# One kernel, two layers of attention and feed-forward: the first two phases put in one block, and the expert's rows gathered instead of scattered

## The chip, the cores and the metric

The kernel runs on one core of a Trainium2 chip. The metric is the device time of one execution in microseconds (us). The kernel before takes 649.71 us, the median of three runs (648.31, 649.71 and 651.97).

## What is computed

The input is x of shape (16, 256, 128), 4096 tokens of 128 numbers, and four residual steps follow one another:

```python
x = x + _L0_attn_ref(_layernorm(x, axis=-1), ...)   # gated linear attention, 16 heads of 8
x = x + _L0_ffn_ref(_layernorm(x, axis=-1), ...)    # 8 experts, one per token, and a shared expert
x = x + _L1_attn_ref(_layernorm(x, axis=-1), ...)   # conv, silu, decaying state, gate
x = x + _L1_ffn_ref(_layernorm(x, axis=-1), ...)    # FP4-quantised gated feed-forward
```

The change is all in the second step. Its router picks one expert for each token, and the token enters that expert multiplied with the sigmoid of its score:

```python
scores_aE = x_aD @ router_DE
vals_aK, idx_aK = jax.lax.top_k(scores_aE, 1)
gates_Ea = jax.nn.sigmoid(masked_aE).T
routed_in_EaD = gates_Ea[:, :, None] * x_aD[None, :, :]
mid_EaF = silu(routed_in_EaD @ w1_eDF) * (routed_in_EaD @ w3_eDF)    # F = 352
routed_out_EaD = mid_EaF @ w2_eFD
shared_aD = silu(x_aD @ ws1_DF) * (x_aD @ ws3_DF) @ ws2_FD
out_aD = shared_aD + routed_out_EaD.sum(axis=0)
```

## The kernel before

Tokens lie in 32 tiles of 128 (one tile is 128 partitions by 128 numbers). The work is four functions, `phase_a` to `phase_d`, one after the other. Each opens an `nc.Block()`, in which every engine has its own list of instructions and semaphores order them; at the end of a block all engines and their DMAs have to be done before any engine goes on. There is no planner: the order on each engine is written out by hand. `run_skewed(engine, body, first, lo, hi, last)` issues `body(j)` for all j, the middle ones in a hardware loop. `done(engine, semaphore, j, n, per, ago)` waits until step j - ago has been counted.

`phase_a` (L193) does the attention and the second layer norm, one batch of 256 tokens (two tiles) per step of a software pipeline over 16 batches. In a step TensorE scores keys against queries (`products`, L821, into the four banks of `ps_a`), ScalarE, VectorE and GpSimd copy and mask them into `at` (`copied` L423, `masked` L540, `cut` L361), TensorE multiplies with the values (`values`, L745), and `finish` (L843 to L845) forms the output. Then the normed rows `xn2s` are made on ScalarE (`normed`, L432), copied to `xn2` by GpSimd (`copy_xn2`, L368), transposed to `xn2T`, and the router's scores of the batch are taken (`scores`, L727). At the end of its queue SyncE loads the weights of the next phases and stores zeros over the whole of `xg_dram`, 40 stores of 128 rows (L329).

`phase_b` (L924) does two things side by side. TensorE runs the shared expert over 8 groups of 512 tokens: three steps `f` of six matmuls of 512 columns (L188 to L190, into two buffers each of `ps_1` and `ps_3`), and `down`, 24 matmuls of 128 rows (L1147). ScalarE takes silu (L1032), VectorE the product (L1107). Meanwhile the tokens are sorted by expert. VectorE finds each token's expert as a one-hot row (L1067 to L1076), TensorE counts (`count_and_rank`, L1134 to L1137), VectorE turns counts into `pos`, the row at which each token lies when tokens are sorted by expert and each expert's part is padded to whole slots of 128 (L1083 to L1091; 40 slots). GpSimd multiplies each tile with its gate (`gated`, L994) and scatters its rows to `xg_dram` at `pos` with an indirect DMA (L1002), 32 tiles one after the other, and then waits for all of them (L1007). The expert weights `w13` are split into a high and a low part, `expert_high` on ScalarE (L1014) and `expert_low` on VectorE (L1061).

`phase_c` (L1173) runs the experts over 20 pairs of slots in 22 steps. SyncE loads the rows of a pair from `xg_dram` (L1221), two pairs ahead; TensorE transposes them (L1359), multiplies with w1 and w3 of the slot's expert (`up`, L188 to L190), transposes the product (L1389) and multiplies with w2 (L1367); VectorE copies out (L1311) and SyncE stores to `yg_dram` (L1225). GpSimd splits the weights of the next layer here (L1261 to L1267), and VectorE quantises weights in steps 1 to 3 (`prepare`). `phase_d` (L1397) gathers rows from `yg_dram` and adds them to x (L1493), and does the second layer.

Of the kernel before, what the change touches and what calls it, by code (L numbers as in the profile page):

```python
# [28 lines left out]
P = 128  # L29
# [49 lines left out]
def apart(eng):  # L79

    eng.nop(nofuse=True)
# [21 lines left out]
def constants():  # L103
# [13 lines left out]
            np.broadcast_to(EXPERTS - np.arange(EXPERTS, dtype=np.float32), (P, EXPERTS)),  # L117
        ],
# [10 lines left out]
def build(nc, io, out):  # L129
    ctx = ExitStack()  # L130
    with ctx:
# [3 lines left out]
        def sb(name, shape, dt=F32):  # L135
# [12 lines left out]
            "xg_dram": nc.dram_tensor("xg_dram", (SLOTS * P, D), F32, kind="Internal").ap(),  # L148
            "yg_dram": nc.dram_tensor("yg_dram", (SLOTS * P, D), F32, kind="Internal").ap(),
            "pos": sb("pos", [P, T], U32),  # L150
            "slot_expert": sb("slot_expert", [1, SLOTS], I32),
        }
        with ExitStack() as mid:
# [4 lines left out]
            g["small"] = sbm("small", [P, SLOTS + EXPERTS])  # L158
# [4 lines left out]
            with ExitStack() as early:  # L163
                def sbe(name, shape, dt=F32):
                    return early.enter_context(nc.sbuf_tensor(name, shape, dt))

                g["xn2"] = sbe("xn2", [P, T, D])
                g["xn2T"] = sbe("xn2T", [P, T * P])
                g["scores"] = sbe("scores", [P, EXPERTS, T])
                phase_a(nc, io, g)  # L170
                phase_b(nc, io, g)
# [13 lines left out]

def split_product(nc, to, left, right, start=True, stop=True):
# [6 lines left out]
def phase_a(nc, io, g):  # L193
    x, mask, ones, halves = g["x"], g["mask"], g["ones"], g["halves"]
    ident = mask[:, 2, :]
    with ExitStack() as ctx:
# [9 lines left out]
        ws = sb("ws", [P, 2, F])  # L206
        rope = sb("rope", [P, 2, N])
        block = sb("block", [P, P])
        wall = sb("wall", [P, 4 * P])
        wallp = sb("wallp", [P, 2, 4 * P], F32R)  # L210
        wload = sb("wload", [P, 2, P])
# [28 lines left out]
        zero = sb("zero", [P, D])  # L240
# [9 lines left out]
        xn2s = sb("xn2s", [P, 2, D])  # L250
        xn2t = sb("xn2t", [P, N])

# [4 lines left out]
        ps_m = bank("ps_m", [P, 512])  # L257

# [14 lines left out]
        s_xn2p, s_xn2t, s_xn2c, s_sc, s_scc = sem("s_xn2p"), sem("s_xn2t"), sem("s_xn2c"), sem("s_sc"), sem("s_scc")  # L273
# [16 lines left out]
        def _(sp):  # L290
# [17 lines left out]

            def body(j):
                done(sp, s_qs, j)  # L310
                apart(sp)
                done(sp, s_a, j, n=8, per=8, ago=2)
                if j.off == 0:
                    sp.wait_ge(s_zero, 2)
                for h in range(4):
                    sp.dma_start(qx[h::4, j.par, h, :, :].rearrange("p c n -> p (c n)"),
                                 qs[h::4, j.par, :, :].rearrange("p c n -> p (c n)")).then_inc(s_qx[j.par], 16)

            run_skewed(sp, body, 0, 2, 14, B - 1)

            sp.dma_start(g["small"][:, :], io["c_small"]).then_inc(g["s_w"], 16)
            for f, (f0, fn) in enumerate(FT):
                sp.dma_start(g["ws2"][0:fn, f, :], io["L0_ffn_ws2_FD"][f0:f0 + fn, :]).then_inc(g["s_w"], 16)
# [3 lines left out]
            sp.wait_ge(s_zero, 3)  # L327
            for s in range(SLOTS):
                sp.dma_start(g["xg_dram"][P * s:P * (s + 1), :], zero[:, :]).then_inc(g["s_w"], 16)  # L329
            sp.wait_ge(g["s_w"], 16 * (4 + 3 + SLOTS))  # L330

        @blk_.gpsimd
        def _(pool):
# [4 lines left out]
            nc.gpsimd.memset(zero[:, :], 0.0).then_inc(s_zero, 1)  # L338
# [24 lines left out]

            def copy_xn2(b):
                if not live(b):
                    return
                done(pool, s_xn2, b)
                nc.gpsimd.tensor_copy(g["xn2"][:, f_tiles(b), :], xn2s[:, :, :]).then_inc(s_xn2c, 1)  # L368
# [27 lines left out]
            def body(j):  # L396
                copy_xn2(j + -2)
# [11 lines left out]
            run_skewed(pool, body, -3, 3, 13, B + 1)  # L409

        @blk_.scalar
        def _(act):
# [5 lines left out]
            def copied(b, t, r):  # L418
# [4 lines left out]
                nc.scalar.activation(at[:, t, r, :, :], ps_a[:, r, :, :], ACT.Copy).then_inc(s_copied, 1)  # L423

# [83 lines left out]
            def body(j):  # L508
                copied(j, 1, 3)
                copied(j, 1, 1)  # L510
                normed(j + -1, xn2s, rstd2, shift2, s_nb2, (s_xn2p, s_xn2c), s_xn2)
# [7 lines left out]
                copied(j + 1, 0, 1)  # L519
                normed(j + 3, xn, rstd, shift, s_nb1, (s_xnTp,), s_xn)  # L520
# [4 lines left out]
            run_skewed(act, body, -3, 3, 13, B)  # L525

        @blk_.vector
        def _(dve):
# [128 lines left out]
            def body(j):  # L657
# [29 lines left out]
                lower(j + 1)  # L687

            run_skewed(dve, body, -2, 4, 14, B + 1)

            dve.wait_ge(s_ws, 32)
            nc.vector.tensor_copy(g["ws1"][:, 0, :, :], ws[:, :, :]).then_inc(s_prep_dve, 1)
            dve.wait_ge(s_prep_dve, 4)
            nc.vector.tensor_tensor(g["ws1"][:, 1, :, :], ws[:, :, :], g["ws1"][:, 0, :, :].bitcast(F32), ALU.subtract)

        @blk_.tensor
        def _(pe):
# [95 lines left out]
            def transposes2(b):  # L793
# [8 lines left out]
                for t in range(2):  # L802
                    last = nc.tensor.transpose(ps_t[:, tile(t)], xn2s[:, t, :], ident)
# [69 lines left out]
            run_skewed(pe, body, -2, 4, 14, B + 1)  # L873
# [50 lines left out]
def phase_b(nc, io, g):  # L924

    x, mask, ones = g["x"], g["mask"], g["ones"]
    scores, xn2, xn2T = g["scores"], g["xn2"], g["xn2T"]
    small, ws1, ws2 = g["small"], g["ws1"], g["ws2"]
    GROUPS, GT = T // 4, 4 * P
    with ExitStack() as ctx:  # L930
        def sb(name, shape, dt=F32):
            return ctx.enter_context(nc.sbuf_tensor("b_" + name, shape, dt))

        def sem(name):
            return ctx.enter_context(nc.semaphore("b_" + name))

        def bank(name, shape):
# [909 lines left out]
```

## Time and profile before

| | |
|---|---|
| median of three runs | 649.71 us |
| the profiled execution | 653.99 us, its span 652.3 us, mean granted clock of TensorE 0.936 |
| TensorE busy with matmuls | 551.6 us (85%) |
| TensorE busy with weight loads | 445.9 us (68%), beside matmuls |
| VectorE busy | 438.3 us (67%) |
| GpSimd busy | 355.2 us (54%) |
| ScalarE busy | 307.8 us (47%) |
| DMA | 28.12 MB, mean 43 GB/s |

The profile is one execution, taken by the hardware. Its times are counted from the start of the span. PE is TensorE (PEld its weight loads), DVE is VectorE, ACT is ScalarE, POOL is GpSimd, SP is SyncE; a q behind a name is the engine's sequencer or queue. A row of the timeline gives the start, the length, the engine, the line of the kernel, the operation, out<-in and how many were merged; a bracket at its end is how long the engine had been idle and who released it. Matmuls overlap one another, so that rates are read from starts, not from the length of one. The granted clock is a share of TensorE's full clock of 2.4 GHz; 0.50 is the level of 1.2 GHz.

### The profile page before, as it was taken

Reading aid. Unit: us, or ns where it says so; the run is one execution under the profiler, and the core shown is the slowest. Engines: PE = TensorE matmul, PEld = TensorE weight load, DVE = VectorE, ACT = ScalarE, POOL = GpSimd, SP = SyncE. Lnnn points to the kernel's source line nnn. Section 1 sums busy time; section 2 is a strip of 40 time slices with the busy share of each in tenths; the row PEclk is TensorE's granted clock in tenths of the full one; section 3 lists DMA queues with packets and bytes.
Section 4 is the critical chain, followed back from the end, with each engine's and each line's share of the span. In section 5 each row is a group of like instructions: output and inputs, shape, how many; then the busy total and the mean of one; then the engine's idle time right before and its main releaser. Section 6 shows DMA issues by size and latency. Waiting matters only on the chain. (4 is left out here: it accounts for less than half of the span.)

```text
span 652.3 us, 15280 instructions
## 1 busy us (share of the span) xinstructions
PE 551.6 (85%) x4468; PEld 445.9 (68%) x4469; DVE 438.3 (67%) x1172; ACT 307.8 (47%) x862; POOL 355.2 (54%) x550
## 2 busy tenths in 40 slices
PE   2799999999999379991799999278899999999965
PEld 1457676776776258871689999266778778778754
DVE  2678999999885155552284343126899899899883
ACT  1356666666574224430245444124545645655632
POOL 4468877878776248885400000445667767764221
PEclk9999999999999659996699999778899999999987
DMA  7000000000004551111422111110011011010000
GB/s 200 16 20 33 19 26 25 16 32 16 23 26 108 158 196 34 32 34 43 116 58 57 56 56 40 33 16 10 10 32 18 16 32 17 16 25 15 10 17 16
DMA packets 41686, 28.12 MB, mean 43 GB/s; under 512 B 5232, under 2 KB 38192, under 8 KB 41648
## 3 DMA queue, kind: packets, MB, share of 16 engines
q1 hardware_dynamic: 36016, 23.46, 12.2%
q0 software_dynamic: 5632, 4.20, 3.7%
q8 instruction: 19, 0.31, 0.2%
q14 instruction: 19, 0.16, 0.1%
HBM read 14.01 MB, written 9.44 MB: 36 GB/s over the span
## 5 line engine op out<-in xcount | busy, mean ns | idle before, releaser
L821 PE MATMUL a_ps_a<-a_qx,a_kt 32*128 32x512 f32 x512 | 70.8, 643 | 1.2 <-DMA a_qx<-a_qs 1.0
L1493 POOL DMA_INDIRECT x<-yg_dram,pos x32 | 58.1, 1815 | 11.9 <-issue 11.9
L895 POOL TENSOR_TENSOR d_hq<-d_fh_v,d_fh_scale 128x352 f32<-128x352 f32 x32 | 27.9, 889 | 57.6 <-DVE d_fh_v L921 57.6
L361 POOL TENSOR_SCALAR_AFFINE_SELECT a_at<-a_at 128x512 f32<-128x512 f32 x80 | 50.5, 650 | 11.8 <-ACT a_at L423 11.5
L1317 DVE TENSOR_TENSOR c_hid<-c_act,c_ps 128x352 f32<-128x352 f32 x40 | 20.7, 520 | 44.4 <-ACT c_act L1274 35.7
L423 ACT ACTIVATE a_at<-a_ps_a 128x512 f32<-128x512 f32 x80 | 44.5, 600 | 11.7 <-PE a_ps_a L821 10.1
L1498 POOL MEMSET d_hs<- 128x256 f32 x1 | 0.3, 311 | 88.3 <-POOLq L1177 88.3
L821 PEld LDWEIGHTS a_ps_a<-a_qx,a_kt 32*128 32x128 f32 x512 | 32.1, 192 | 17.9 <-issue 17.2
L1274 ACT ACTIVATE c_act<-c_ps 128x352 f32<-128x352 f32 x40 | 18.5, 463 | 49.6 <-PE c_ps L190 49.2
L1002 POOL DMA_INDIRECT xg_dram<-xn,pos x32 | 35.3, 1104 | 11.9 <-DVE pos L1091 6.2
L188 PE MATMUL d_ps_A<-d_xnT,wmix 128*128 128x256 f32 x128 | 38.4, 300 | 1.6 <-DVE d_xnT L1672 0.9
L540 DVE TENSOR_TENSOR a_at<-a_ps_a,mask 128x512 f32<-128x512 f32 x48 | 32.7, 684 | 8.6 <-PE a_ps_a L821 7.3
L190 PE MATMUL d_ps_A<-d_xnT,wmix 128*128 128x256 f32 x128 | 37.2, 290 | 0.0
L189 PE MATMUL d_ps_A<-d_xnT,wmix 128*128 128x256 f32 x128 | 37.2, 290 | 0.0
L745 PE MATMUL a_ps_o<-a_at,a_vpad 128*32 128x128 f32 x1024 | 34.6, 276 | 0.0
L1107 DVE TENSOR_TENSOR b_hid<-b_act,b_ps 128x512 f32<-128x512 f32 (+1 forms) x24 | 16.4, 683 | 25.8 <-ACT b_act L1032 25.8
L188 PE MATMUL c_ps<-w13p,c_xT 128*128 x80 | 30.8, 385 | 2.0 <-issue 1.0
L1032 ACT ACTIVATE b_act<-b_ps 128x512 f32<-128x512 f32 (+1 forms) x24 | 14.3, 596 | 38.4 <-PE b_ps L190 37.9
L1367 PE MATMUL c_ps_y<-w,c_hidT 128*128 (+1 forms) x240 | 31.6, 281 | 0.8 <-ACT c_hidT L1291 0.8
L393 POOL TENSOR_TENSOR a_kt<-a_e,a_rope 128x512 f32<-128x512 f32 x16 | 20.4, 1276 | 21.6 <-ACT a_e L447 21.6
L1367 PEld LDWEIGHTS c_ps_y<-w,c_hidT 128*128 128x128 f32 (+1 forms) x240 | 28.3, 191 | 3.0 <-issue 1.9
L1816 PEld LDWEIGHTS d_ps_G<-d_wd,d_hqT 128*128 128x128 f32 (+1 forms) x192 | 23.8, 199 | 8.6 <-issue 5.5
(274 smaller groups left out, 1807.3 us busy)
## 6 DMA issues: line engine op xcount, KB each, us to landing
a_qx<-a_qs SPq DMA_DIRECT2D x64, 64.0 KB, 1.9
b_w<-in_L_ffn_w_eDF_dram SPq DMA_DIRECT2D x2, 1408.0 KB, 8.1
xg_dram<-a_zero SPq DMA_DIRECT2D x40, 64.0 KB, 1.6
c_rows<-xg_dram SPq DMA_DIRECT2D x20, 128.0 KB, 2.1
yg_dram<-c_y SPq DMA_DIRECT2D x20, 128.0 KB, 1.8
out_dram<-x SPq DMA_DIRECT2D x16, 128.0 KB, 1.9
w<-in_L_ffn_w_eFD_dram SPq DMA_DIRECT2D x2, 512.0 KB, 5.1
x<-in_L_attn_x_dram SPq DMA_DIRECT2D x1, 768.0 KB, 5.7
```

The source lines that it names most:

```text
L188: nc.tensor.matmul(to, left(0), right(0), start=start, stop=False)
L189: nc.tensor.matmul(to, left(0), right(1), start=False, stop=False)
L190: return nc.tensor.matmul(to, left(1), right(0), start=False, stop=stop)
L361: nc.gpsimd.affine_select(at[:, t, r, :, :], at[:, t, r, :, :], pattern=[[0, 4], [1, P]], compare_op=ALU.is_ge, fill=0.0, base=0, channel_ ...
L423: nc.scalar.activation(at[:, t, r, :, :], ps_a[:, r, :, :], ACT.Copy).then_inc(s_copied, 1)
L540: nc.vector.tensor_tensor(at[:, t, r, :, :], ps_a[:, r, :, :], mask[:, 0:1, :].to_broadcast([P, 4, P]), ALU.mult).then_inc(s_masked, 1)
L745: last = nc.tensor.matmul(ps_o[32 * r:32 * r + 32, tile(t)], vpad[:, b.par, t, c0:c0 + 32], at[:, t, r, h, :], start=(t == 0 and h == 0), ...
L821: last = nc.tensor.matmul(ps_a[:, r, :, :], kt[rows, b.par, c_, tile(t)], qx[rows, b.par, :, c_, tile(t)], start=(c_ == 0), stop=(c_ == 1))
L895: return eng.tensor_tensor(self.by(to), self.by(self.v[:, :]), self.spread(self.scale), ALU.mult)
L1002: nc.gpsimd.indirect_dma_start(out=g["xg_dram"][:, :], out_offset=bass.IndirectOffsetOnAxis(ap=g["pos"][:, t:t + 1], axis=0), in_=xn2[:, t ...
L1367: last = nc.tensor.matmul(ps_y[:, t, :], hidT[0:fn, f.par, t, n, :], w2[0:fn, e_out[t], n, :], start=(n == 0), stop=(n == 2))
L1493: nc.gpsimd.indirect_dma_start(out=x[:, t, :], out_offset=None, in_=g["yg_dram"][:, :], in_offset=bass.IndirectOffsetOnAxis(ap=g["pos"][:, ...
```

## The change

- `phase_a` and `phase_b` become one function, `phase_ab`, in one block. The three last steps of the attention pipeline are written out by hand, with the first groups of the shared expert between them (`up(n, f)` is one step of the six matmuls, `down(n, half)` half of the 24). The shared expert uses PSUM banks and SBUF of the attention again: `ps_1` and `ps_3` are `ps_a`, the routing tables lie in `kt` and `qs`, the expert weights (a ring of five) in `at`.
- `xg_dram`, its 40 stores of zeros, the tiles' gating and the scatter are gone. In their place the normed rows are stored as they are, unsorted, to `xn2_dram` by SyncE, one store of 256 rows per batch from one of two buffers `xn2s`; GpSimd's copy to `xn2` goes.
- A table says which token lies in each place of each slot. VectorE splits `pos` into slot and place, and compares both against constants, which gives one-hot matrices `slot_high` (32 tiles by 40) and `slot_low` (32 tiles by 128, in four parts). GpSimd multiplies `slot_high` with the gate and with the token's number. 32 products on TensorE (`slots`) sum them to `slot_token` and `slot_gate` for the 40 slots.
- `gather` fetches the 256 rows of a pair with two indirect DMAs from GpSimd, into one of four buffers `rows`: pairs 0 to 3 in `phase_ab`, pairs 4 to 19 in `phase_c`. There VectorE multiplies them with `slot_gate` into the old two buffers before TensorE's transposes. VectorE's loop in `phase_c` is written out. SyncE loads no rows.
- `expert_low` goes from VectorE to GpSimd. The split of the shared expert's weights on VectorE goes from the end of `phase_a` to its step 3.

```diff
+def gather(nc, g, k):
+    for t in range(2):
+        nc.gpsimd.indirect_dma_start(
+            out=g["rows"][:, k % 4, t, :], out_offset=None, in_=g["xn2_dram"][:, :],
+            in_offset=bass.IndirectOffsetOnAxis(ap=g["slot_token"][:, 2 * k + t:2 * k + t + 1], axis=0),
+        ).then_inc(g["s_rows"][k % 4], 16)
...
     @blk_.sync
+            def store(b):
...
+                done(sp, s_xn2, b)
+                sp.dma_start(xn2_rows[:, f_tiles(b), :], xn2s[:, b.par, :, :]).then_inc(s_xn2s[b.par], 16)
...
             def body(j):
+                store(j + -4)
...
-            for s in range(SLOTS):
-                sp.dma_start(g["xg_dram"][P * s:P * (s + 1), :], zero[:, :]).then_inc(g["s_w"], 16)
...
     @blk_.gpsimd
-                copy_xn2(j + -2)
...
+            expert_low(0)
+            pool.wait_ge(s_pos, 1)
...
+            nc.gpsimd.tensor_tensor(slot_high[:, :, SLOTS:], slot_high[:, :, 0:SLOTS],
+                                    gate.unsqueeze(2).to_broadcast(by_slot), ALU.mult).then_inc(s_one, 1)
...
+            nc.gpsimd.tensor_tensor(slot_high[:, :, 0:SLOTS], slot_high[:, :, 0:SLOTS],
+                                    small[:, SLOTS + EXPERTS + P:].unsqueeze(2).to_broadcast(by_slot), ALU.mult).then_inc(s_part, 1)
+            for e_ in range(1, 4):
+                expert_low(e_)
+            pool.wait_ge(s_tab, 2)
...
+            for k in range(2):
+                gather(nc, g, k)
+            for e_ in range(4, EXPERTS):
+                expert_low(e_)
+            for k in range(2, 4):
+                gather(nc, g, k)
...
     @blk_.scalar
...
+            gated_up(0, 0)
+            squares(Seq(B - 1))
+            gated_up(0, 1)
+            gated_up(0, 2)
+            gated_up(1, 0)
+            scored(Seq(B - 2))
+            normed2(Seq(B - 1))
...
     @blk_.vector
...
+            for n in range(2, GROUPS):
+                for f in range(3):
+                    hidden(n, f)
+                    if f == 0 and n + 1 < GROUPS:
+                        token_low(n + 1)
+                    if (n, f) == (2, 2):
+                        positions()
+                    if (n, f) == (3, 0):
+                        slot_rows()
+                    if (3, 1) <= (n, f) <= (4, 1):
+                        slot_places(3 * n + f - 10)
+                    if (n, f) == (4, 2):
+                        slot_experts()
+                    if (n, f) == (5, 1):
+                        slot_table()
+                add(n - 1)
...
     @blk_.tensor
...
+            transposes2(Seq(B - 2))
+            up(0, 0)
+            values(Seq(B - 1), 1)
+            up(0, 1)
+            finish(Seq(B - 1))
+            up(0, 2)
+            up(1, 0)
+            scores(Seq(B - 2))
+            down(0, 0)
+            up(1, 1)
+            down(0, 1)
+            transposes2(Seq(B - 1))
+            up(1, 2)
+            scores(Seq(B - 1))
+            up(2, 0)
+            down(1, 0)
+            up(2, 1)
+            count_and_rank()
+            down(1, 1)
+            up(2, 2)
+            group(3)
+            group(4)
+            for part in range(4):
+                slots(part)
+            group(5)
...
 def phase_c(nc, io, g):
...
     @blk_.gpsimd
+            def rows_for(k):
+                done(pool, s_rg, Seq(k), ago=4)
+                gather(nc, g, k)
...
     @blk_.vector
+                if live(j + 2):
+                    k = j + 2
+                    dve.wait_ge(g["s_rows"][k.off % 4], 32 * (k.off // 4 + 1))
+                    done(dve, s_xp, k, ago=2)
+                    for t in range(2):
+                        c0 = 2 * k.off + t
+                        last = nc.vector.tensor_scalar(rows[:, k.par, t, :], g["rows"][:, k.off % 4, t, :],
+                                                       g["slot_gate"][:, c0:c0 + 1], None, ALU.mult)
+                    last.then_inc(s_rg, 1)
```

## Rows read from the trace of the kernel before

**Rows 1.** By stage: length, busy PE PEld DVE ACT POOL, clock, DMA share, GB/s.

```profile
27.00:197.00 170.00, 165.41 (x1929) 117.84 (x1929) 148.59 (x386) 109.06 (x320) 129.34 (x235) 1.00 0.06 23
209.90:232.20 22.30, 7.61 (x96) 6.01 (x93) 5.89 (x17) 6.38 (x17) 6.88 (x17) 0.67 0.58 153
232.20:242.60 10.40, 10.23 (x26) 7.24 (x26) 6.96 (x16) 2.61 (x5) 4.07 (x6) 0.55 0.78 273
242.60:297.10 54.50, 52.80 (x318) 43.70 (x318) 29.82 (x46) 21.53 (x36) 48.67 (x54) 1.00 0.11 33
297.10:309.80 12.70, 0.03 (x1) 0.03 (x1) 1.49 (x2) 0.00 (x0) 5.88 (x8) 0.59 0.15 46
309.80:323.00 13.20, 8.70 (x31) 7.16 (x31) 2.72 (x6) 2.80 (x7) 4.07 (x3) 0.63 0.53 144
323.00:413.00 90.00, 86.37 (x612) 79.88 (x610) 41.90 (x84) 40.86 (x134) 3.35 (x2) 1.00 0.18 50
```

**Rows 2.** Timeline where phase_a ends and phase_b begins.

```profile
208.25 20.87 SPq L329 DMA_DIRECT2D xg_dram<-a_zero  x40
209.91 0.61 PE L727 MATMUL a_ps_m<-a_router,a_xn2t 128*128 128x8 f32 x4
...
215.24 0.60 PE L843 MATMUL a_ps_m<-ones,a_sq 128*128 128x1 f32 x4 [0.99 <-ACT a_sq L478]
...
230.80 0.60 DVE L1067 TENSOR_REDUCE b_best<-scores 128x32 f32<-128x256 f32 x1 [10.46 <-PEq L196]
...
231.68 1.28 ACT L1032 ACT_TABLE_LOAD   x1
...
232.17 0.79 PE L188 MATMUL b_ps<-b_tokens,ws 128*128 128x512 f32 x1 [7.19 <-DVE b_tokens L1055]
```

**Rows 3.** Timeline where phase_b ends and phase_c begins, and its last product.

```profile
294.11 2.94 PE L1147 MATMUL b_ps_y<-ws,b_hid 128*128 128x128 f32 x24 [1.40 <-DVE b_hid L1107]
...
302.38 0.96 POOL L1002 DMA_INDIRECT xg_dram<-xn,pos  x1 [0.30 <-issue]
307.71 0.88 SPq L1221 DMA_DIRECT2D c_rows<-xg_dram  x2
...
309.77 0.69 PE L1359 MATMUL c_ps_t<-mask,c_rows 128*128 128x128 f32 x2 [12.72 <-DMA c_rows<-xg_dram]
...
324.44 1.50 PE L1367 MATMUL c_ps_y<-w,c_hidT 128*128 x12
...
410.38 1.60 PE L1367 MATMUL c_ps_y<-w,c_hidT 128*128 x12 [0.83 <-ACT c_hidT L1291]
...
414.73 0.31 POOL L1498 MEMSET d_hs<- 128x256 f32 x1 [88.30 <-POOLq L1177]
```

**Rows 4.** Costliest groups of the page: the indirect DMAs of GpSimd, scatter and gather.

```profile
L1493 POOL DMA_INDIRECT x<-yg_dram,pos x32 | 58.1, 1815 | 11.9 <-issue 11.9
...
L1002 POOL DMA_INDIRECT xg_dram<-xn,pos x32 | 35.3, 1104 | 11.9 <-DVE pos L1091 6.2
```

**Rows 5.** Timeline of the shared expert: the same half of down in two groups.

```profile
279.84 1.60 PE L1147 MATMUL b_ps_y<-ws,b_hid 128*128 128x128 f32 x12
...
286.98 1.60 PE L1147 MATMUL b_ps_y<-ws,b_hid 128*128 128x128 f32 x12
```

**Rows 6.** Instructions of single lines: ns min/median/max, first and last start, forms.

```profile
L895 POOL TENSOR_TENSOR d_hq<-d_fh_v,d_fh_scale x32: 777/889/1002, 463.7 to 644.3; 128x352 f32<-128x352 f32 x32
...
L895 DVE TENSOR_TENSOR wq<-c_w_v,c_w_scale x1: 1326/1326/1326, 336.6 to 336.6; 128x1120 f32<-128x1120 f32 x1
...
L1267 POOL TENSOR_TENSOR wmix<-c_wtap,wmix x1: 2927/2927/2927, 323.5 to 323.5; 128x1280 fp32r<-128x1280 f32 x1
```

**Rows 7.** Timeline: one scan on VectorE beside GpSimd's multiply, and one without.

```profile
192.29 1.29 POOL L393 TENSOR_TENSOR a_kt<-a_e,a_rope 128x512 f32<-128x512 f32 x1 [0.77 <-ACT a_e L447]
...
192.64 1.21 DVE L603 TENSOR_TENSOR_SCAN a_c<-ones,a_de,a_e 128x128 f32<-128x128 f32 x1
...
194.28 0.48 DVE L603 TENSOR_TENSOR_SCAN a_c<-ones,a_init,a_e 128x128 f32<-128x128 f32 x1
```

More of the change, by code:

```diff
@@ L151, in build @@
             "slot_expert": sb("slot_expert", [1, SLOTS], I32),
+            "slot_token": sb("slot_token", [P, SLOTS], U32),
+            "slot_gate": sb("slot_gate", [P, SLOTS]),
+            "rows": sb("rows", [P, 4, 2, D]),
+            "s_rows": [sem(f"s_rows{n}") for n in range(4)],
         }
@@ new lines, in _ @@
+            done(dve, s_x2, Seq(B - 1))
+            norm_stats(Seq(B - 1), stats2, s_st2)
+            norm_aggr(Seq(B - 1), stats2, mv2, s_st2, s_nb2, s_ln2)
+            hidden(0, 2)
+            hidden(1, 0)
+            hidden(1, 1)
+            add(0)
+            token_low(2)
+            hidden(1, 2)
+            one_hot()
+            for n in range(2, GROUPS):
+                for f in range(3):
+                    hidden(n, f)
+                    if f == 0 and n + 1 < GROUPS:
+                        token_low(n + 1)
[10 more added lines that the diff above has]
+                add(n - 1)
@@ L696, in _ @@
+            add(GROUPS - 1)
         @blk_.tensor
@@ new lines, in group, with count_and_rank @@
+            def group(n):
+                for f in range(3):
+                    up(n, f)
+                    if f < 2:
+                        down(n - 1, f)
+            def count_and_rank():
+                pe.wait_ge(s_hot, 2)
+                to = ps_r.rearrange("p e t -> p (e t)")
+                nc.tensor.matmul(ps_n, ones[:, :], hot[:, :, T - 1], start=True, stop=False)
+                nc.tensor.matmul(ps_n, ones[:, :], before[:, :, T - 1], start=False, stop=True)
+                nc.tensor.matmul(to, mask[:, 1, :], padded[:, 1:], start=True, stop=False)
+                nc.tensor.matmul(to, ones[:, :], before.rearrange("p e t -> p (e t)"),
+                                 start=False, stop=True).then_inc(s_r, 1)
@@ new lines, in slots @@
+            def slots(part):
+                if part == 0:
+                    pe.wait_ge(s_part, 1)
+                pe.wait_ge(s_pos, part + 2)
+                for t in range(8 * part, 8 * part + 8):
+                    last = nc.tensor.matmul(ps_s, slot_low[:, t, :], slot_high[:, t, :], start=(t == 0), stop=(t == T - 1))
+                if part == 3:
+                    last.then_inc(s_tab, 1)
+            run_skewed(pe, body, -2, 4, 14, B - 2)
+            scores(Seq(B - 3))
+            values(Seq(B - 1), 0)
```

530 lines of the change are left out of this document (269 added, 261 removed).

## Prediction

> **What bounds the kernel now.** I read the busy time by stage first. From 27 to 197 us and from 323 to 413 us TensorE is busy 97% and 96% of the time at full clock: the attention and the experts are bound by TensorE, and so is the shared expert between 242.6 and 297.1 (52.8 of 54.5) [rows 1]. Between these stand two seams where it hardly works. In the first, from 209.9 to 232.2, it is busy for 7.6 us of 22.3, and then runs at a clock of 0.55 until 242.6. In the second it does nothing for 12.7 us (297.1 to 309.8) and then has 8.7 us of work in 13.2, at 0.63 [rows 1].
>
> The timeline says who holds each seam. In the first, VectorE has long been idle when it starts phase_b at 230.80, 10.5 us after its last work: SyncE is storing zeros until 208.25 + 20.87 = 229.1, and the block can't end before they land. The first matmul of phase_b is at 232.17 [rows 2]. In the second, TensorE is done at 294.11 + 2.94 = 297.05, while GpSimd issues its last scatter at 302.38 and the next block starts at 307.71; the first transpose waits 12.7 us, and the first product with w2 (step 2 of phase_c) comes at 324.44 [rows 3]. GpSimd's 32 scatters take 1.10 us each with 0.37 us before them [rows 4], and the 32 multiplies by the gate lie between; that chain is longer than TensorE's part of phase_b.
>
> **First seam and shared expert.** Both kernels have the same work on TensorE up to the router product at 209.91 [rows 2]. I add what it has to do from there. What is left of the attention was 7.61 us of busy time at a mean clock of 0.67 [rows 1]; part ran at the lower level, and I take 6.5. A group of the shared expert takes 286.98 - 279.84 = 7.14 us [rows 5]; eight are 57.1, and the last half waits 1.4 for VectorE [rows 3]. Phase_b took 297.05 - 232.17 = 64.9 us, which is 6.4 more than 57.1 + 1.4; 10.4 us at 0.55 cost 4.7 of that [rows 1], and 1.7 are counting and waits, which stay. New are the 32 products of the slot table. A float32 product runs as two instructions here: 64 instructions, as 24 take 2.94 us [rows 3] 0.12 each, at most 7.8; they move 80 columns and not 128, so 7.5. Together 74.2 us.
>
> To this come stalls. The last batch is still a chain over four engines; now matmuls lie between its links, but `finish` stands in TensorE's queue ahead of `up(0, 2)` and waits for ScalarE's square, as it does before for 0.99 us [rows 2]; I count three such waits (the normed rows, the square, the one-hot rows) at 1.2 us, 3.6. `Square` and `Tanh` now stand between two `Silu`. Before, one table load of 1.28 us does for the change from one to the other [rows 2]. The reload for the gate's tanh (two loads, 2.6 us) falls beside VectorE's `positions`, which is longer: nothing. If the square needs one too, it costs up to 2.6 us.
>
> The second stall is VectorE in groups 3 and 4. Its usual work is 29.82 us in 54.5 [rows 1], 3.9 a group, 3.0 without `expert_low`. It gets `positions` (12 small operations, an estimate of 3.4), `slot_rows` with 1280 elements and four `slot_places` with 1024, which by the 1.33 us of a spread multiply of 1120 elements [rows 6] are 1.5 and 1.2 each. That is 2 x 3.0 + 3.4 + 1.5 + 4.9 = 15.8 us against TensorE's 14.3, which alone costs 1.5. Beside it GpSimd does two multiplies of 1280 elements, 2.9 us each [rows 6]. A scan on VectorE that meets GpSimd's multiply takes 1.21 us and 0.48 without it, ending with it (193.85 and 193.58) [rows 7], so VectorE can lose anything from 0 to 5.8. I take 3, and 4.5 for this stall. `slots` waits for the last part. The Trainium skill, page "SBUF — State Buffer", section "Who interferes with whom", says that a VectorE instruction with two inputs in SBUF and a GpSimd instruction that reads SBUF exclude each other for the whole instruction; the trace agrees for this scan. By that rule the whole 5.8 us would be lost, and the sum would be 2.8 us higher.
>
> TensorE so ends at 209.9 + 74.2 + 3.6 + 4.5 = 292.2, against 297.05.
>
> **Is GpSimd done by then?** After the table it issues four gathers, four `expert_low` and four more gathers. A gather without adding is not in the trace. The nearest rows are the scatter, 1.10 + 0.37 = 1.47, and the gather that adds, 1.82 + 0.37 = 2.19 [rows 4]; I take 1.6, nearer to the one that doesn't add. `expert_low` has 704 elements, between 0.89 us for 352 and 2.93 for 1280 [rows 6], 1.66. 12.8 + 6.6 = 19.4 us stand against TensorE's 14.3 + 2.9 + 1.4 and some 3 of group 5's start, 21.6: done 2 us before it, or at 2.19 each 2.5 us after it.
>
> **Second seam.** No scatter has to end, and the pairs' rows are there. After TensorE VectorE adds the last group, 0.7 us (1.49 us for two operations there [rows 1]), then the block ends. The end of a block with indirect DMAs cost 307.71 - 303.34 = 4.4 us [rows 3], part of it the wait for the last scatter; the one to phase_d comes 2.7 us after the last product, with a copy and a store in it [rows 3]. Bounds are 0 and 4.4; I take 2. Phase_c starts at 295.0 instead of 307.7.
>
> From there to the first product with w2 it was 16.7 us [rows 3]. TensorE's work in it is 8.70 us at 0.63, 5.5 at full clock [rows 1]; with the multiply by the gate, a transpose and two copies ahead of it 7.5 us at full clock, and 13 at 0.50. In the second seam before, a mean of 0.59 over 12.7 us [rows 1] means that the upper level held for 2.3 us after the last matmul; the new gap is about 4 us, so I expect a fall, and take 11.5. Step 2 then begins at 306.5 instead of 324.4: 17.9 us earlier.
>
> **Third phase.** A pair takes (410.38 - 324.44) / 19 = 4.52 us [rows 3]. GpSimd's two gathers are 3.2 us of it (4.4 at the dearest price), and it may run four pairs ahead; its 7.4 us of other work [rows 1] fits in that lead. VectorE is busy 41.9 of 90 us [rows 1], 2.1 a pair, and gets two multiplies, some 0.5. If a gather is late, VectorE waits for it, and behind it in its queue stand `prepare` and the next pair's copies, so TensorE two steps later. I take 0, up to 3 for a gather late at the start. SyncE's loads go at no gain: at pairs other than the first they were hidden. The last phases are as they were.
>
> **First phase.** Off go 16 copies on GpSimd (busy 129 of 170 us) and on come 16 stores in SyncE's queue ahead of the queries' DMAs, whose data are older by then; VectorE (149 of 170) gets the shared weights' split, 1.4 us, in step 3. TensorE is busy 165 of 170 [rows 1], so these can move it by some -2 to +2; I take 0.
>
> **Sum.** The profiled execution took 653.99 us with a span of 652.3, 4.3 above the median of 649.71. The saving is taken off both: span 634.4, execution 636.1, median 631.8.
>
> **The rivals.** *A clean seam:* VectorE keeps up (-4.5), the clock stays up at the start of phase_c (-4), the block's end costs 0.5 (-1.5): 27.9 saved, 621.8. For it speaks that VectorE and GpSimd have few common operations with two inputs; against it the 15.8 us against 14.3.
>
> *The seam is only moved:* the whole of GpSimd's multiplies is lost (+2.8), the square's table load (+2.6), gathers at 2.19 and 4.4 us for the block's end (2.5 + 4.4 behind TensorE's end instead of 2.8: +4.1), phase_c's start at the lower level (+1.5): 6.9 saved, 642.8. The scan's row speaks for the first of these, the 4.4 us for the third.
>
> *Slower:* phase_c becomes bound by GpSimd's 32 gathers. From 295 to the end of the last product at 412.0 are 117 us; less 7.4 of other work it breaks even at 3.4 us a gather (it begins to bind at 2.9). At 4.0 it would be 7.4 + 128 = 135.4 us, 18.4 more than before: 668. The trace's dearest is 2.19. The same page warns, in "SBUF: two separate sides", that GpSimd can't write descriptors while VectorE runs a copy-like operation in a two-port mode, and the new multiply by the gate is one. No row here shows it on an indirect DMA; by it a gather would wait for at most a 0.5 us multiply.
>
> **How the numbers follow.** My forecast has 0.53, the clean seam 0.18, the moved seam 0.20, the slower case 0.05; 0.04 are left for something not seen. The range goes from the clean seam to a little beyond the moved one: 621 to 645. A measurement of this kernel can tell 0.5% (3.3 us) from no change. Faster by more: 0.88, within: 0.05, slower: 0.07.
>
> **What would show it.** TensorE's last product with ws2 near 292 (284 if there were no stalls); the matmuls of `slots` close together for some 7.5 us; `slot_places` over 1.3 us where they meet GpSimd's multiplies; a gather of 1.1 to 1.8 us; phase_c's first transpose at about 296 and its first w2 product at 306; TensorE's clock near 1.00 from 210 to 290; pairs of 4.52 us. The prediction is wrong if a gather takes 3 us, or if TensorE in phase_c waits for `rows`.

## The result, and the profile after

The changed kernel takes 663.64 us (median of 4 runs, 662.30 to 664.89) against 650.84 for the kernel before (4 runs): a ratio of 1.021, 95% interval 1.018 to 1.023. It is slower by 13 us, where 18 us less were forecast. The profiled execution took 662.30 us with a span of 660.6, which is 8.3 us above the span of the kernel before; the other 4.5 of the 13 us are spread between executions (the profiled one is the shortest of its four, and that of the kernel before, at 653.99, is longer than all four runs beside it), and the account below is one of the two profiled spans.

The stage windows are read first, as in [rows 1]. Columns: stretch, its length, busy time of PE, PEld, DVE, ACT and POOL, granted clock, DMA share, GB/s.

```profile
27.00:197.00 170.00, 165.47 (x1928) 117.84 (x1929) 149.33 (x388) 108.89 (x320) 125.42 (x222) 1.00 0.09 32
209.90:232.20 22.30, 20.53 (x175) 16.81 (x173) 12.53 (x27) 11.72 (x25) 4.87 (x14) 1.00 0.58 159
232.20:290.00 57.80, 52.00 (x324) 44.18 (x323) 36.95 (x54) 17.53 (x30) 28.26 (x19) 0.97 0.10 29
290.00:305.80 15.80, 8.71 (x47) 7.06 (x46) 6.18 (x17) 3.88 (x11) 6.63 (x9) 0.89 0.46 119
305.80:420.30 114.50, 87.28 (x604) 77.73 (x602) 48.53 (x113) 40.32 (x129) 34.39 (x30) 1.00 0.16 37
```

The first phase is as it was. The first seam is gone: TensorE is busy 20.5 of its 22.3 us at full clock, where it had been busy 7.6. The loss is in the last line. The third phase has the same work for TensorE, 87.3 us against 86.4, but 114.5 us to do it in and not 90. The clock is 1.00 there, so it isn't the clock.

The timeline at the second seam answers to [rows 3]. Columns: start, length, engine, line, operation, and the idle time before it with what ended it.

```profile
287.96 2.94 PE L1176 MATMUL a_ps_o<-ws,a_hid 128*128 128x128 f32 x24 [1.40 <-DVE a_hid L876]
288.08 0.94 POOL L193 DMA_INDIRECT rows<-xn_dram,slot_token  x1 [0.30 <-issue]
290.94 0.69 DVE L880 TENSOR_TENSOR x<-x,a_ps_o 128x512 f32<-128x512 f32 x1 [2.44 <-PE a_ps_o L1176]
291.92 0.53 POOL L1367 MEMSET c_wraw<- 128x512 f32 x1 [2.90 <-POOLq L211]
...
292.64 0.44 PE L1484 MATMUL c_ps_t<-mask,c_rows 128*128 128x128 f32 x2 [1.74 <-DVE c_rows L1439]
...
305.81 1.50 PE L1492 MATMUL c_ps_y<-w,c_hidT 128*128 x12
```

The shared expert ends at 290.90, phase_c starts at 291.92 and the first product with w2 is at 305.81, 18.6 us earlier than the 324.44 of before. Up to here the change gave what was forecast.

From there the products with w2 show the loss. These are rows of one period of the third phase, from the transposes of one step to those of the next:

```profile
375.49 0.44 PE L1484 MATMUL c_ps_t<-mask,c_rows 128*128 128x128 f32 x2 [1.50 <-DVE c_rows L1439]
375.70 0.94 POOL L193 DMA_INDIRECT rows<-xn_dram,slot_token  x1 [4.23 <-DVE c_rows L1439]
375.77 1.51 PE L1492 MATMUL c_ps_y<-w,c_hidT 128*128 x12
...
379.89 0.32 PE L203 MATMUL c_ps<-w13p,c_xT 128*128 x1
380.25 0.46 ACT L1389 ACTIVATE c_act<-c_ps 128x352 f32<-128x352 f32 x1 [0.23 <-PE c_ps L203]
380.74 0.52 DVE L1432 TENSOR_TENSOR c_hid<-c_act,c_ps 128x352 f32<-128x352 f32 x1 [1.10 <-ACT c_act L1389]
381.18 0.48 DVE L1439 TENSOR_SCALAR c_rows<-rows,slot_gate 128x128 f32<-128x128 f32 x2
381.79 0.43 PE L1484 MATMUL c_ps_t<-mask,c_rows 128*128 128x128 f32 x2 [1.58 <-DVE c_rows L1439]
```

TensorE works from 375.49 to 380.21 and then stands for 1.58 us. What it stands for is a chain over three engines that starts with its own last matmul: ScalarE's silu, VectorE's product, VectorE's two multiplies by the gate, and only then the transposes of pair j+2. The waits of TensorE between 300 and 415 us (in total, times, longest) say how much that is:

```profile
PE c_ps_t L1484 <- DVE c_rows L1439: 28.2, 18, 2.1
```

The forecast's measure of a pair was (last product - first) / 19: it is (418.92 - 305.81) / 19 = 5.95 us now and was 4.52, so the 19 take 27.2 us more, and 16 of the 18 waits lie in them. The other two, 1.50 us each at 300.27 and 305.54, stand ahead of the first w2 product, so the waits account for 28.2 - 3.0 = 25.2 of the 27.2 us; where the other 2.0 lie is not settled. The first 16 periods take (407.25 - 305.81) / 16 = 6.34 us; in the kernel before, with the 17th product at 398.75, they took (398.75 - 324.44) / 16 = 4.64. The last three have no transposes ahead of them, and take 4.25, 4.33 and 3.09 us, as they did before:

```profile
394.73 1.60 PE L1492 MATMUL c_ps_y<-w,c_hidT 128*128 x12
401.02 1.51 PE L1492 MATMUL c_ps_y<-w,c_hidT 128*128 x12
407.25 1.53 PE L1492 MATMUL c_ps_y<-w,c_hidT 128*128 x12
411.50 1.60 PE L1492 MATMUL c_ps_y<-w,c_hidT 128*128 x12
415.83 1.60 PE L1492 MATMUL c_ps_y<-w,c_hidT 128*128 x12
418.92 1.60 PE L1492 MATMUL c_ps_y<-w,c_hidT 128*128 x12 [0.83 <-ACT c_hidT L1406]
...
423.28 0.31 POOL L1623 MEMSET d_hs<- 128x256 f32 x1 [39.16 <-POOLq L1293]
```

The account closes: 18.6 us won up to the first w2 product, 27.2 lost in the third phase, and from the start of phase_d 660.6 - 423.28 = 237.3 us against 237.6. That is a span of 652.3 - 18.6 + 27.2 - 0.3 = 660.6.

### The profile page after: what moved, and what is told of

It reads as the page before. It is cut to its first block and busy times, and to the rows that moved or that the text cites. A ratio compares the mean times of both kernels' runs of the same rounds, so it can differ in the third digit from the quotient of the medians.

```text
span 660.6 us, 15223 instructions
## 1 busy us (share of the span) xinstructions
PE 555.4 (84%) x4532; PEld 448.4 (68%) x4533; DVE 455.0 (69%) x1215; ACT 308.1 (47%) x862; POOL 351.6 (53%) x519
## 5 line engine op out<-in xcount | busy, mean ns | idle before, releaser
L193 POOL DMA_INDIRECT rows<-xn_dram,slot_token x40 | 40.2, 1004 | 61.2 <-DVE c_rows L1439 45.8
L1432 DVE TENSOR_TENSOR c_hid<-c_act,c_ps 128x352 f32<-128x352 f32 x40 | 20.8, 521 | 46.2 <-ACT c_act L1389 46.2
L525 ACT ACTIVATE a_at<-a_ps_a 128x512 f32<-128x512 f32 x80 | 44.5, 599 | 11.5 <-PE a_ps_a L1097 9.9
L1097 PEld LDWEIGHTS a_ps_a<-a_qx,a_kt 32*128 32x128 f32 x512 | 32.0, 192 | 17.7 <-issue 17.1
L1389 ACT ACTIVATE c_act<-c_ps 128x352 f32<-128x352 f32 x40 | 18.6, 464 | 49.7 <-PE c_ps L203 49.7
L1484 PE MATMUL c_ps_t<-mask,c_rows 128*128 128x128 f32 x40 | 8.7, 300 | 31.3 <-DVE c_rows L1439 31.3
L651 ACT ACTIVATE a_act<-a_ps_a 128x512 f32<-128x512 f32 (+1 forms) x24 | 14.3, 595 | 43.5 <-PE a_ps_a L203 43.5
L876 DVE TENSOR_TENSOR a_hid<-a_act,a_ps_a 128x512 f32<-128x512 f32 (+1 forms) x24 | 16.4, 682 | 25.8 <-ACT a_act L651 25.7
L462 POOL TENSOR_TENSOR a_kt<-a_e,a_rope 128x512 f32<-128x512 f32 x16 | 20.4, 1277 | 21.6 <-ACT a_e L561 21.6
```

What stands on the lines that cost most here:

```text
L193: nc.gpsimd.indirect_dma_start(out=g["rows"][:, k % 4, t, :], out_offset=None, in_=g["xn2_dram"][:, :], in_offset=bass.IndirectOffsetOnAxi ...
L1097: last = nc.tensor.matmul(ps_a[:, r, :, :], kt[rows, b.par, c_, tile(t)], qx[rows, b.par, :, c_, tile(t)], start=(c_ == 0), stop=(c_ == 1))
```

## The experiments

The theory, the ring: at the end of VectorE's step j, the multiply for pair j+2 stands behind the two products of pair j, and TensorE's step j+1 begins with the transposes of pair j+2. So the latency of silu, product and multiply is paid on TensorE once a pair. The rival, cost: the multiplies, or the gathers that they wait for, are simply more work than the third phase has room for. It was the forecast's own "slower" case, with gathers of over 2.9 us.

**The multiply ahead of the products.** The same instructions, in another order. Two further kernels, below, have each multiply twice (once into a buffer that nobody reads), in the late and in the early place.

```
-                if live(j):
-                    for t in range(2):
-                        done(dve, s_act, j, n=t + 1, per=2)
-                        ...
                 if live(j + 2):
                     ...
                     last.then_inc(s_rg, 1)
+                if live(j):
+                    for t in range(2):
+                        done(dve, s_act, j, n=t + 1, per=2)
+                        ...
```

> The changed kernel with one edit: in the third phase VectorE multiplies the rows of pair j+2 by the gate ahead of its two products of pair j instead of behind them. Theory (the wait): behind the products the multiply closes a ring from one step to the next, up(j,1) on TensorE, silu on ScalarE, product and multiply on VectorE, and then the transposes that stand first in TensorE's next step; in the trace of the changed kernel the transposes wait 31.3 us for the multiply, and a pair takes (418.92 - 305.81) / 19 = 5.95 us instead of 4.52. Moved ahead, a pair should be back at 4.5 to 4.6 us, the transposes should wait under 5 us in all, and the time should fall by some 27 us from 663.6, to 636. Rival (the gathers): GpSimd's indirect DMAs, their descriptors or their landing hold the pairs up, and the multiply only passes that on; then a pair stays near 5.9 us and the time within 3 us of 663.6.

Measured: 637.59 us (4 runs, 635.37 to 639.81) beside 651.42 for the kernel before, ratio 0.978 (0.973 to 0.983). In the trace the transposes' wait is nearly gone, and 11 pairs in a row (331.66 to 382.02) take 4.58 us each. Here are the same row of the waits and the dearest early step; columns of the second as in the timeline above:

```profile
PE c_ps_t L1484 <- DVE c_rows L1433: 4.9, 2, 3.5
```

```profile
320.01 3.29 POOL L1380 TENSOR_TENSOR wmix<-c_wtap,wmix 128x1280 fp32r<-128x1280 f32 x1
...
320.57 3.92 DVE L1260 TENSOR_TENSOR wq<-c_w_v,c_w_scale 128x1120 f32<-128x1120 f32 x1
...
325.60 0.44 PE L1484 MATMUL c_ps_t<-mask,c_rows 128*128 128x128 f32 x2 [3.55 <-DVE c_rows L1433]
```

The w2 products take 398.24 - 305.63 = 92.6 us against 113.1 in the changed kernel and 85.9 before: the order gave back 20.5 of the 27.2 us, where the theory had all of them. (The medians differ by 26, but the two spans by 660.6 - 638.0 = 22.6.) What is left is `prepare`: three of its operations stand in VectorE's queue in one step, and one of 1.33 us [rows 6] takes 3.92 beside GpSimd's multiply of 3.29. The first four pairs took 5.87, 6.03, 8.34 and 5.79 us.

**Each multiply twice, late.**

```
                     for t in range(2):
                         c0 = 2 * k.off + t
+                        nc.vector.tensor_scalar(spare[:, t, :], g["rows"][:, k.off % 4, t, :],
+                                                g["slot_gate"][:, c0:c0 + 1], None, ALU.mult)
                         last = nc.vector.tensor_scalar(rows[:, k.par, t, :], ...
```

> The changed kernel with the gate's multiply of each pair done twice in its late place (the first time into a spare buffer): 0.5 us more of VectorE's work a pair. Theory (the wait): it lies on the ring, so each pair takes 0.45 to 0.55 us more, 6.4 to 6.5, and the time is some 9 us above 663.6. Rival (the gathers): VectorE is busy 48.5 of 114.5 us in the third phase and has room; a pair stays at 5.95 and the time within 2 us.

Measured: 675.50 us (one run), 12 above the changed kernel. The first 16 periods of the w2 products (309.24 to 419.55) take 6.89 us each against 6.34 in the changed kernel (305.81 to 407.25): 0.55 us more, for two multiplies of some 0.24 us. Over 16 that is 8.8, the 9 that the theory had; another 3.4 us lie ahead of the first product, where the theory had none.

**Each multiply twice, early.** The same lines in the early place.

> The early multiply of e1_early, done twice. Theory (the wait): ahead of the products it lies beside TensorE's first half of the step and off the ring, so the second multiply costs nothing: a pair within 0.1 us of e1_early's and the time within 2 us of it. Rival (VectorE is simply too busy in the third phase, wherever the multiply stands): a pair takes 0.3 us or more longer than in e1_early and the time is 5 us or more above it.

Measured: 637.63 us (one run), the same as with single multiplies. Ten pairs (332.10 to 377.83) take 4.57 us. This one execution flatters it: its shared expert ended 4.8 us earlier than in the kernel with single multiplies (last product at 282.85 against 287.64), in code that is the same in both. Measured on the w2 products alone, the doubling costs 95.7 - 92.6 = 3.1 us, all of it in the early pairs, where VectorE is full. So the same extra half microsecond a pair costs 0.55 us of each period in one place and nothing in the other, once `prepare` is over. The cost theory falls. Each of these two kernels ran once, so this reading rests on the stretches inside their traces.

**The ring in the kernel before.** To see it without the gathers and without the joined block, the kernel before got it alone: SyncE loads a pair into an extra buffer, and VectorE copies it (a multiply by 1.0) into the buffer that TensorE transposes, at the end of its step or ahead of the products.

```
-                sp.dma_start(rows[:, j.par, :, :], ...
+                sp.dma_start(rows_in[:, j.par, :, :], ...
...
+                if live(j + 2):
+                    k = j + 2
+                    dve.wait_ge(s_rows[k.par], k.half(16, 16))
+                    done(dve, s_xp, k, ago=2)
+                    for t in range(2):
+                        last = nc.vector.tensor_scalar(rows[:, k.par, t, :], rows_in[:, k.par, t, :], 1.0, None, ALU.mult)
+                    last.then_inc(s_rg, 1)
```

> The kernel before, with SyncE's loads of rows as they are, but into a buffer of their own, from which VectorE copies each pair in two operations of 128x128 at the end of its step j (for pair j+2), the place that the gate's multiply has in the changed kernel. No gather, no merged block. Theory (the wait): the copy alone makes the ring; a pair takes 5.9 to 6.0 us and the time rises by some 27 us, from 650.8 to 678. Rival (the gathers, or anything else of the change in the third phase): the copy is 0.5 us of work on an engine busy 2.1 of 4.5 us a pair, so a pair stays at 4.5 to 4.6 and the time within 3 us of 650.8.

> The kernel before with VectorE's copy of the rows as in e4_before_copy_late, but ahead of the two products of the step. Theory (the ring is made by the place, not by the work): a pair in the steady part takes 4.5 to 4.6 us, as in the kernel before, and the time is within 3 us of 651.4. Rival (an operation more on VectorE and a buffer more between load and transposes cost wherever they stand): a pair takes over 5 us and the time is 10 us or more above it.

Measured: the late copy 681.11 us (4 runs), ratio 1.047 (1.043 to 1.052), the early one 655.13 (8 runs), ratio 1.006 (1.003 to 1.009). The w2 products take 110.5 us with the late copy (328.69 to 439.19) and 86.2 with the early one (323.74 to 409.98), 85.9 before. One wait of each period with the late copy, and TensorE's total (300 to 415 us, of which 13.1 are the seam):

```profile
378.15 1.60 PE L1376 MATMUL c_ps_y<-w,c_hidT 128*128 x12
...
384.04 0.44 PE L1368 MATMUL c_ps_t<-mask,c_rows 128*128 128x128 f32 x2 [1.38 <-DVE c_rows L1325]
384.32 1.52 PE L1376 MATMUL c_ps_y<-w,c_hidT 128*128 x12
```

```profile
PE c_ps_t L1368 <- DVE c_rows L1325: 40.6, 18, 13.1
```

A copy of 0.35 us for a pair, put in that place, makes a period of 4.64 us one of 6.18 (328.69 to 427.53, 16 of them) in a kernel that has nothing else of the change. Of the 29.7 us that the late copy costs, 24.6 lie in the w2 products and 4.3 ahead of the first (328.69 against 324.44). The early copy came out 4 us above the kernel before, a little more than the 3 expected; the third phase of its profiled execution has only 0.3 of that, and where the rest lies isn't settled.

**`prepare` spread out.** On top of the early multiply, one operation of `prepare` for each step and not three.

```
-                if 1 <= j.off < LO:
-                    for n in range(3 * j.off - 3, 3 * j.off):
-                        prepare(n)
+                if 3 <= j.off < 12:
+                    prepare(j.off - 3)
```

> e1_early with the nine operations of prepare (the next layer's weights on VectorE, 0.2 to 1.3 us each) spread, one at the end of each of steps 3 to 11, instead of three at the end of each of steps 1 to 3. In e1_early the first four pairs still take 5.9, 6.0, 8.3 and 5.8 us, some 7.7 us more than four at 4.57; in the third of these VectorE's last operation takes 3.92 us beside GpSimd's split of weights (3.29 us), and 1.33 in the kernel before. Theory: blocks of 3 to 6.6 us at the end of a step hold the row multiply and the low parts of the next one; spread, the first pairs come down to 4.6 to 5.2 us and the time falls by 5 to 8 us from 637.6, to some 631. Rival (the early pairs are slow from the clock, the loads or the landing of rows): the first four pairs keep their 7 us, and the time stays within 2 us.

Measured: 628.78 us (4 runs, 627.29 to 629.78) beside 651.16, ratio 0.965 (0.962 to 0.968), the lowest median of this study. The w2 products take 86.3 us (300.30 to 386.62) against 92.6 with the early multiply alone: 6.3 us is what the spreading gives. The other 2.5 of the 8.8 between the medians can't be put down to it: the profiled execution of the kernel without it has ScalarE idle for 4.64 us just ahead of the first w2 product, which the trace puts down to no engine and for which TensorE waits 3.79 us, and two of its four runs were 4 us faster than the other two. One steady step, with the transposes not waiting:

```profile
341.23 0.47 DVE L1433 TENSOR_SCALAR c_rows<-rows,slot_gate 128x128 f32<-128x128 f32 x2
341.39 0.47 ACT L1389 ACTIVATE c_act<-c_ps 128x352 f32<-128x352 f32 x1 [2.06 <-PE c_ps L203]
...
341.89 0.52 DVE L1441 TENSOR_TENSOR c_hid<-c_act,c_ps 128x352 f32<-128x352 f32 x1 [0.19 <-ACT c_act L1389]
...
342.74 0.38 PE L1483 MATMUL c_ps_t<-mask,c_rows 128*128 128x128 f32 x2
```

The multiply lies in the time in which VectorE waits for silu.

**The slot table's multiplies on VectorE.** On top of the spread kernel, the two multiplies of 1280 elements go from GpSimd to VectorE.

```
-            nc.gpsimd.tensor_tensor(slot_high[:, :, SLOTS:], ...
-            nc.gpsimd.tensor_tensor(slot_high[:, :, 0:SLOTS], ...
+                nc.vector.tensor_tensor(slot_high[:, :, SLOTS:], ...
+                nc.vector.tensor_tensor(slot_high[:, :, 0:SLOTS], ...
```

> e6_spread with the two multiplies of slot_high (1280 elements) on VectorE, behind slot_rows, instead of GpSimd. In the changed kernel the first two slot_places took 2.99 and 2.76 us, with GpSimd's multiplies from 246.9 to 252.5 beside them, and the last two 1.21. Theory (VectorE and GpSimd exclude each other in such operations): all four take 1.2 us, the two multiplies 1.5 each; 3.3 us of blocking goes and 3.0 of work comes, so the end of the shared expert moves by less than 1.5 us and the time by less than 2. Rival (the first two are slow for another reason, such as their place or the writes into that buffer): they stay over 2.5 us, and the end is 3 us or more later.

Measured: 629.44 us (one run). First the spread kernel's timeline, then this one's:

```profile
245.22 2.35 POOL L496 TENSOR_TENSOR a_vpad<-a_vpad,a_kt 128x1280 f32<-128x1280 f32 x1 [6.15 <-DVE a_vpad L914]
245.66 2.99 DVE L919 TENSOR_TENSOR a_qx<-a_kt,small 128x1024 f32<-128x1024 f32 x1
...
247.64 3.20 POOL L499 TENSOR_TENSOR a_vpad<-a_vpad,small 128x1280 f32<-128x1280 f32 x1
249.16 2.76 DVE L919 TENSOR_TENSOR a_qx<-a_kt,small 128x1024 f32<-128x1024 f32 x1
...
253.95 1.21 DVE L919 TENSOR_TENSOR a_qx<-a_kt,small 128x1024 f32<-128x1024 f32 x1
```

```profile
243.41 1.49 DVE L911 TENSOR_TENSOR a_vpad<-a_vpad,a_kt 128x1280 f32<-128x1280 f32 x1
244.93 2.86 DVE L914 TENSOR_TENSOR a_vpad<-a_vpad,small 128x1280 f32<-128x1280 f32 x1
...
248.31 1.21 DVE L919 TENSOR_TENSOR a_qx<-a_kt,small 128x1024 f32<-128x1024 f32 x1
250.04 1.21 DVE L919 TENSOR_TENSOR a_qx<-a_kt,small 128x1024 f32<-128x1024 f32 x1
```

With no multiply of GpSimd beside them, the four `slot_places` take 1.21 or 1.22 us; beside one they take 2.99 and 2.76, 3.3 us lost in all. The change costs as much as it saves: VectorE has the two multiplies to do (1.49 and 2.86, the second beside GpSimd's `expert_low`), and from `slot_rows` to the shared expert's last product it takes 46.2 us instead of 42.6. That is more than the theory's 1.5 and as much as the rival had, though not for the rival's reason: TensorE stood 5.4 us for one product of VectorE, and its granted clock was 0.50 from 248 to 252 us.

**`slot_places` two thirds of a group later.** On top of the spread kernel, VectorE's four `slot_places` come later (and with them the two steps behind them, `slot_experts` and `slot_table`), and the matmuls of `slots` between those of groups 4 and 5.

```
-                    if (3, 1) <= (n, f) <= (4, 1):
-                        slot_places(3 * n + f - 10)
+                    if (4, 0) <= (n, f) <= (5, 0):
+                        slot_places(3 * n + f - 12)
...
+            up(5, 0)
+            down(4, 0)
+            up(5, 1)
             for part in range(4):
                 slots(part)
-            group(5)
+            down(4, 1)
+            up(5, 2)
```

> e6_spread with the four slot_places after the products (4,0) to (5,0) instead of (3,1) to (4,1), and the 32 table products on TensorE between up(5,1) and down(4,1) instead of ahead of group 5. In the changed kernel groups 3 and 4 take 20.5 us instead of 14.3, because products of the shared expert stand behind the blocked slot_places. Theory: without the block 4 to 6 us of that go, the shared expert ends at 285 to 287 instead of 290.9; the table is ready a little later against TensorE, so GpSimd's gathers end the block, at best 3 us earlier: the time is 2 to 4 us below e6_spread. Rival (GpSimd's chain alone sets the end of the block): less than 1 us is won.

Measured: 631.95 us (4 runs, 628.27 to 632.31), ratio to before 0.968 (0.964 to 0.972): its range overlaps the spread kernel's (627.29 to 629.78), and the 2 to 4 us less that the theory had did not come.

```profile
283.80 2.94 PE L1176 MATMUL a_ps_o<-ws,a_hid 128*128 128x128 f32 x24 [1.40 <-DVE a_hid L876]
...
286.79 0.69 DVE L880 TENSOR_TENSOR x<-x,a_ps_o 128x512 f32<-128x512 f32 x1 [2.44 <-PE a_ps_o L1176]
287.88 0.94 POOL L193 DMA_INDIRECT rows<-xn_dram,slot_token  x1 [0.30 <-issue]
291.00 0.52 POOL L1371 MEMSET c_wraw<- 128x512 f32 x1 [2.18 <-POOLq L211]
...
291.73 0.69 PE L1487 MATMUL c_ps_t<-mask,c_rows 128*128 128x128 f32 x2 [4.98 <-DVE c_rows L1437]
```

From `count_and_rank` to the last product TensorE takes 52.5 us (231.30 to 283.80) and not 54.6 (231.66 to 286.26). Only part of that can be the new place: two of the four `slot_places` now meet `expert_low` on GpSimd, and take 2.72 and 2.12 us. The granted clock was 1.00 throughout, where in the spread kernel it was 0.58 from 249.3 to 253.2; the kernel with the early multiply done twice, whose code up to here is the spread kernel's, also kept 1.00 and took 53.0 us.

But the later table has moved GpSimd's gathers, and the block now ends behind them: the last one ends at 288.82, and the next block starts 2.18 us on. (A gather lands some 2.6 us after its issue, here 287.88, so its landing falls in that time; no run tells the two apart.) In the spread kernel the last thing was VectorE's addition, with 0.28 us behind it. TensorE's pause grows to 4.98 us, and its transposes come at 0.69 us and not 0.44, with a granted clock of 0.50 from 291.7 to 298.0. In the joined block TensorE and GpSimd end within some 2 us of each other, so shortening TensorE's part alone won nothing.

## Why the prediction was wrong

**What bounds the kernel now** was read rightly; both seams shrank as it said.

**First seam and shared expert**: forecast end of TensorE 292.2, measured 290.90. The 32 products of the table took 7.3 us (forecast 7.5). In the stretch of groups 3 and 4 TensorE waited three times for VectorE, 1.6, 0.9 and 1.8 us, 4.3 in all. That is not the whole stall, for which I had 4.5: from 237.4 to 258.15 the two groups took 20.8 us instead of 14.3, 6.5 more. Behind the third wait the granted clock was 0.50 from 252.0 to 254.9, where I had expected it near 1.00. The multiplies of GpSimd cost VectorE 3.3 us (forecast 3). By the Trainium skill, page "SBUF — State Buffer", section "Who interferes with whom", the two exclude each other for the whole instruction; the trace agrees for each instruction that met a multiply (2.99 and 2.76 us against 1.21), but only two of four met one, so the loss was 3.3 and not 5.8. There was one table load of 1.28 us for `Silu`, none for `Square` or `Tanh` between them: the rival's 2.6 us for it did not come. The last batch's stalls were 22.3 - 20.5 = 1.8 us up to 232.2, where I had 3.6. So the end within 1.3 us of the forecast is partly luck: one stall came out 2 us larger and another 1.8 smaller.

**Is GpSimd done by then?** The gathers took 0.94 us with 0.30 before them, and not 1.6: below both rows that I had put around them [rows 4]. Yet GpSimd ended at 289.02, 1.9 us before TensorE (forecast 2): its first gather could start only when the table was ready, at 271.35, which is 19.6 us before TensorE's end and not 21.6; from there it took 17.7 us (forecast 19.4).

**Second seam**: 2.8 us were forecast between TensorE's end and phase_c, it took 1.02. In these traces the end of the block costs 0.3 where VectorE's addition is last, and 2.2 where a gather is last. The pause of TensorE was 1.74 us and not about 4, and its clock stayed at 1.00 up to 296; it was 0.57 from there to 300. From phase_c's start to the first w2 product it took 13.9 us against 11.5, though the clock was 0.89 and so better than I had it: the ring was already at work there, with waits of 1.5 us for `c_rows`; in the spread kernel the same stretch took 300.30 - 290.22 = 10.1. Together 305.8 against 306.5, by errors of -1.3, -1.8 and +2.4 that cancel: that this point was hit so closely is luck. The sentence that SyncE's loads were hidden at all pairs but the first was wrong: in the kernel before the transposes at 319.04 waited 2.67 us for such a load, so the gathers had something to win there.

**Third phase** is the step that failed, "I take 0". It was off by 27.2 us, and nearly the whole error of the forecast is this one term: 634.4 + 27.2 = 661.6 against a span of 660.6. (Between the medians the error is 31.8; the rest is the scatter between executions named above.) The forecast priced the multiply by VectorE's load (41.9 of 90 us busy, so 0.5 us a pair fits), and asked only what a late gather would do behind it. It never asked what stands *ahead* of the multiply in VectorE's queue, and who takes its result first. SyncE's load, which it replaced, was in no compute engine's queue and came two pairs ahead. The step "so TensorE two steps later" was wrong as well, since the transposes of pair j+2 open TensorE's very next step. Both orders were in the code; from them and the rows of the trace the ring could have been summed: silu 0.46, product 0.52, multiplies 0.48, and up to 0.13 us from one engine to the next, together the 1.58 of one wait. Of the 27.2 us the order of the multiply gave back 20.5; the other 6.7 went only when `prepare` was spread, because the multiply also stands behind the `prepare` of the step before. The forecast had named `prepare` only as something that a late gather would hold up.

**The rivals**: the side that the "slower" case took was right and its mechanism wrong. It had gathers at 3.4 us or more; they were at 0.94, and in the third phase (305.8 to 420.3 us) GpSimd waited for VectorE:

```profile
POOL rows L193 <- DVE c_rows L1439: 43.0, 13, 4.3
```

Its chance of 0.05 was that of one mechanism; the new loop over three engines was not among the rivals at all. The last sentence of the forecast named the sign by which it would be wrong, TensorE waiting for `rows` in phase_c, and that is the row of 28.2 us. With the ring taken away and `prepare` spread, the kernel takes 628.8 us, 3 us below the forecast of 631.8. That supports the other terms of the sum but doesn't prove each: they err in both directions, and spreading `prepare` was no part of the change. With the order alone it takes 637.6.

## What to carry to other kernels

When a change puts a compute engine's operation between a load and its consumer inside a loop, write down for one period what stands ahead of it in its engine's queue and at which point of the next step its result is taken: an engine with half its time free still added the latency of what stood ahead in its queue to a ring. Put such an operation where its engine waits anyway (here ahead of the products, in VectorE's wait for silu), and spread one-time work over steps rather than in threes. Where two engines end a block within a couple of microseconds of each other, look at what the block's end costs behind each before shortening one.

## What the runs showed of the hardware

- An indirect gather without adding takes GpSimd 0.94 us with 0.30 us before it, and lands 2.6 us after its issue. In the changed kernel 35 of the 40 took 0.94 to 0.96, and the two longest 1.86 and 1.80: each began while VectorE was in a `SCALAR_TENSOR_TENSOR` of 1.3 us on 1120 elements. Whether that caused it was not tried.
- A `TENSOR_SCALAR` of VectorE, with one input in SBUF, can be held by GpSimd's multiply as well. In the kernel before with the late copy, a pair of them that takes 0.35 us took 3.15 beside a multiply of 2.85:

```profile
311.20 0.35 DVE L1325 TENSOR_SCALAR c_rows<-c_rows_in 128x128 f32<-128x128 f32 x2
...
318.19 3.15 DVE L1325 TENSOR_SCALAR c_rows<-c_rows_in 128x128 f32<-128x128 f32 x2 [0.76 <-DMA c_rows_in<-xg_dram]
318.41 2.85 POOL L1264 TENSOR_TENSOR c_wtap<-c_win,c_cw 128x1024 f32<-128x1024 f32 x1
```

- The same code up to the shared expert's last product started it between 282.85 and 287.96 us in the profiled executions of five kernels. So one whole time against another can't tell less than some 5 us. Up to 3.5 of them had arisen by `count_and_rank` (229.88 to 233.38). Another 1.6 come behind it, from the clock: in four of the five the granted clock was 0.57 to 0.58 for some 4 us, right behind a wait of TensorE of 1.8 us, and from `count_and_rank` to that product it took 54.6 us; in the fifth the same waits (1.6, 1.0 and 1.9 us) were followed by a clock of 1.00, and it took 53.0. Even a stretch inside a trace has to be read with its clock beside it.
